# Reordering node work inside the sparse passes of a graph network kernel: when ScalarE stages a node set, and where TensorE's product and transposes stand

## The reference

```python
edge_index = jnp.stack([src, dst])
h = jnp.maximum(_layernorm(x, axis=-1), 0.0)
x = x + _L0_gnn_ref(h, ...)   # twice: concat(h @ W1 + b1, segsum((h @ W0 + b0)[src], dst)) @ W2 + b2, then / std
h = jnp.maximum(_layernorm(x, axis=-1), 0.0)
x = x + _L1_gnn_ref(h, ...)   # segsum(h[src] @ W + b, dst) / clip(deg, 1)
h = jnp.maximum(_layernorm(x, axis=-1), 0.0)
x = x + _L2_gnn_ref(h, ...)   # three graph convolutions, each scaled by 1/sqrt(deg) on both sides
h = jnp.maximum(_layernorm(x, axis=-1), 0.0)
x = x + _L3_gnn_ref(h, ...)   # per edge: relu([h[src], h[dst]] @ Wm1 + bm1) @ Wm2 + bm2, masked, segsum; then a node network
return x
```

## Time and profile before

| | |
|---|---|
| median of 3 runs | 7783.07 us |
| the profiled execution | 7780.93 us |
| its span, first to last instruction | 7779.1 us |
| mean granted TensorE clock | 0.961 of full speed |
| PE busy | 6960.1 us (89%) |
| GpSimd busy | 5398.6 us (69%) |
| VectorE busy | 3609.6 us (46%) |
| ScalarE busy | 1612.6 us (21%) |
| dense matmuls L2451 | 27930, 3617.2 us busy |
| gathers L837 | 3295, 3140.2 us busy |

### The profile page before, as it was taken

The page is one execution under the profiler, slowest core; times in us unless marked ns, Lnnn a source line. Parts: engine busy times, 40 slices in busy tenths (PEclk is TensorE's granted clock), DMA queues, the critical chain, the costliest instruction groups (busy, mean ns, idle before and its releaser), DMA issues.

```text
span 7779.1 us, 139548 instructions
## 1 busy us (share of the span) xinstructions
PE 6960.1 (89%) x53778; PEld 5623.6 (72%) x53778; DVE 3609.6 (46%) x7497; ACT 1612.6 (21%) x3217; POOL 5398.6 (69%) x5559
## 2 busy tenths in 40 slices
PE   2999999899989999999999999999987777777787
PEld 1677777787777777777877777777766666666676
DVE  7888988334442333333322333333344444444444
ACT  4777777111110000000000000010111111111111
POOL 0466666677657777677767777677747777777776
PEclk9999999999999999999999999999988999899898
DMA  7334333666565666655665556666545555555554
GB/s 152 116 129 133 132 123 132 187 191 188 182 200 185 198 196 192 206 183 181 191 207 179 185 186 188 205 193 187 185 154 148 146 146 148 143 151 145 149 144 131
DMA packets 568381, 1306.54 MB, mean 168 GB/s; under 512 B 223636, under 2 KB 326359, under 8 KB 560471
## 3 DMA queue, kind: packets, MB, share of 16 engines
q1 hardware_dynamic: 295076, 810.67, 31.5%
q0 software_dynamic: 177744, 371.65, 18.5%
q10 hardware_dynamic: 94948, 115.60, 4.3%
HBM read 1097.44 MB, written 207.42 MB: 168 GB/s over the span
## 4 chain that ended last, share of the span: by engine, by line
PE 53%; POOL 19%; issue 8%; DMA 3%; DVE 3%; ACT 0%; ACTq 0%; SPq 0%; DVEq 0%; POOLq 0%
PE PS L2451 41%; POOL GF L826 19%; PE PS L2431 5%; DMA work<-amat 2%; PE PS L2598 1%; PE PS L2297 1%; PE PS L2306 1%; PE PS L2516 1%; PE PS L2438 1%; PE PS L2316 0%; PE PS L2293 0%; PE PS L2457 0%; PE PS L2292 0%; DVE work L1839 0%; PE PS L2295 0%
## 5 line engine op out<-in xcount | busy, mean ns | idle before, releaser
L2451 PE MATMUL PS<-PARTS,work 128*128 128x288 bf16 x27930 | 3617.2, 288 | 66.9 <-issue 44.9
L2451 PEld LDWEIGHTS PS<-PARTS,work 128*128 128x128 fp8e4 x27930 | 2747.0, 99 | 760.2 <-issue 83.0
L837 POOL DMA_INDIRECT GF<-newparts,SRC x1640 | 1563.5, 953 | 687.9 <-issue 493.9
L837 POOL DMA_INDIRECT work<-newparts,SRC x1655 | 1576.7, 953 | 540.6 <-issue 498.3
L826 POOL DMA_INDIRECT GF<-table,SRC x1563 | 1475.0, 944 | 532.5 <-issue 475.7
L821 POOL DMA_INDIRECT GF<-newparts,SRC x659 | 749.9, 1138 | 505.0 <-PE PS L2538 202.1
L2598 PE MATMUL PS<-PARTS,work 128*128 128x289 bf16 x5586 | 999.0, 289 | 0.0
L1190 ACT ACTIVATE work<-PS 128x396 fp8e4<-128x396 f32 x1824 | 865.5, 500 | 290.3 <-PE PS L2516 246.2
L1913 DVE TENSOR_REDUCE FREE<-PS 128x96 f32<-128x288 f32 x415 | 189.7, 457 | 1431.1 <-PE PS L2431 1419.1
L2378 PE MATMUL PS<-work,QW 128*96 128x512 bf16 x1173 | 395.9, 455 | 427.8 <-DMA GF<-table,SRC 388.6
L1839 DVE TENSOR_TENSOR work<-PS,REL 128x1024 bf16<-128x1024 f32 (+1 forms) x611 | 741.3, 1214 | 0.3 <-issue 0.3
(11 more groups left out here) (293 smaller groups left out, 5892.0 us busy)
## 6 DMA issues: line engine op xcount, KB each, us to landing
work<-amat SPq DMA_DIRECT2D x285, 896.0 KB
work<-amat SPq DMA_DIRECT2D x285, 672.0 KB
work<-in_dst_dram SPq DMA_DIRECT2D x195, 512.0 KB
amat<-work SPq DMA_DIRECT2D x57, 1568.0 KB, 5.8
work<-in_edge_attr_dram SPq DMA_DIRECT2D x195, 384.0 KB
GF<-newparts,SRC POOLq DMA_INDIRECT x2299
PARTS<-newparts SPq DMA_DIRECT2D x35, 1008.0 KB, 10.0
work<-newparts,SRC POOLq DMA_INDIRECT x1655
```

Of the source, the lines that this page charges most:

```text
L837: pool.indirect_dma_start(GP[place_of(g)][:, i, :], None, part_rows[a % 2], bass.IndirectOffsetOnAxis(ap=SRC[:, tile:tile + 1], axis=0)).t ...
L2451: last = pe.matmul(PS[:, dense_bank(d), 0:PQ], AB[m][:, jj * WIN:(jj + 1) * WIN].bitcast(FP8), PARTS[:, j * PQ:j * PQ + PQ], start=(j == 0 ...
```

## The change

Four edits, all in the part that passes 1 to 5 share:

1. In ScalarE's loop the units of a slot are taken with the lowest q first. In the six overlap slots the newer unit's staging so stands ahead of the older one's second part and stores. In the pass with "l2c" (pass 5) the older unit's row stores and first part are issued ahead of both.
2. `PRODUCT_AFTER` of pass 1 goes from 1 to 4: the product stands behind the last piece of its slot, not behind the second.
3. In pass 5 VectorE's chain goes from the start of its slot to the place at which TensorE has the product: behind what VectorE does for pieces 0 and 1 of the slot.
4. In pass 5 TensorE's transposes go from the end of slot q = 1 (behind the gathered group) to slot q = 2, behind the second piece.

```diff
-PRODUCT_AFTER = {"l0b": 1, "l1": 1, "l2a": 1, "l2b": 1, "l2c": 1}
+PRODUCT_AFTER = {"l0b": 4, "l1": 1, "l2a": 1, "l2b": 1, "l2c": 1}
 # ScalarE
-            def step(s, phase, q, half, u):
+            def step(s, phase, q, half, u, begun=False):
...
                 if name == "l2c" and q == 3:
-                    store_rows(s, phase, half, u)
-                    first_part(s, phase, half, u)
+                    if not begun:
+                        rows_and_first(s, phase, half, u)
                     second_part(s, phase, half, u)
                     store_parts(s, phase, half, u)
...
                 for t in range(TURNS * SLOTS):
-                    for half, u, q in units_in(t):
+                    units = units_in(t)
+                    if PHASES[a + 1] == "l2c":
+                        for half, u, q in units:
+                            if q == 3:
+                                rows_and_first(S, a + 1, half, u)
+                    for half, u, q in sorted(units, key=lambda unit: unit[2]):
                         if q == 0 and half == 0:
                             act.wait_ge(d_add, a * DB + HEAD + SIDE * (u + 1) + 1)
                         if q == 0 and half == 1:
                             act.wait_ge(f_acc, a * GG + SLOTS * (u + 1) + UNIT_AT - SKIP + 2)
-                        step(S, a + 1, q, half, u)
+                        step(S, a + 1, q, half, u, begun=True)
 # VectorE
+                def first_halves(units):
+                    for half, u, q in units:
+                        if q == 1:
+                            step(S, a + 1, q, False, half, u)
+
                 def slot(t):
...
-                    for half, u, q in units_in(t):
-                        step(S, a + 1, q, False, half, u)
-                    for piece in pieces:
+                    units = units_in(t)
+                    for half, u, q in units:
+                        if q != 1:
+                            step(S, a + 1, q, False, half, u)
+                    if not pieces:
+                        first_halves(units)
+                    for k, piece in enumerate(pieces):
                         d, m = divmod(piece, AC)
                         if m == TURN_AT and d:
                             add_block(d - 1, max(0, t - SKIP))
                         if m == AC - 1:
                             sum_parts(d)
+                        if k == min(PRODUCT_AFTER[PHASES[a + 1]], len(pieces) - 1):
+                            first_halves(units)
 # TensorE
-                if after and (q == 2 and name in ("l1", "l2a", "l2b") or q == 1 and name == "l2c"):
+                if after and q == 2 and name in ("l1", "l2a", "l2b"):
                     turned(phase, half, u)
...
                     for half, u, q in units_in(t):
                         if q == 1:
                             step(S, a + 1, 0, True, half, u)
+                        if q == 2 and PHASES[a + 1] == "l2c":
+                            turned(a + 1, half, u)
```

More of the change, by code:

```diff
@@ L2349, in unit @@
                     for after in (False, True):
+                        if after and q == 2 and PHASES[phase] == "l2c":
+                            turned(phase, half, u)
                         step(s, phase, q, after, half, u)
```

## The result

The changed kernel takes 7731.76 us (median of 6 runs, 7721.56 to 7738.24) against 7781.36 us (6 runs) for the kernel before: a ratio of 0.9935, 95% interval 0.9922 to 0.9948, so 0.65% or some 50 us faster. A second comparison on another occasion gave 0.9930 (0.9916 to 0.9944).

The account below looks back on a forecast made before the run. Took GpSimd's gathers to bound passes 2 to 4 and TensorE passes 1 and 5; 24.7 + 7.9 + 5.8 + 21.9, less 2.5 and 3, plus 3.6 gives 58.4 us, so 7724 us median, range 7707 to 7751.

Parts of the forecast that it names:

- What bounds the passes: Passes 2 to 4 bound by GpSimd's gathers (823 us for 82 groups), passes 1 and 5 by TensorE.
- Pass 1, staging 14.2 us and clock 13.5 us: Pass 1: TensorE's product waits 14.2 us for ScalarE's staging in six places, 13.5 us slower clock behind; both go.
- Edit 3, 7.9 us: Pass 5: TensorE's wait for VectorE's sum over parts, 7.9 us in three places, goes.
- Pass 5, staging 10.5 us: Pass 5: TensorE's wait for ScalarE's staging in the six slots, 10.5 us, goes with edit 1.
- Edit 4, 5.8 us less 2.5 for the turned window: Pass 5: transposes' waits for the chain, 5.8 us, go; the turned window then waits 2.5 us (0 to 6).
- Clock in pass 5, 8.4 us: Pass 5: 8.4 of 10.1 us lost to clock falls hang on waits the change touches, and come back.
- Counts, 3 us: Passes 1 and 5: a faster TensorE waits 3 us (0 to 12) for the counts' DMA.
- Pass 5 as a whole: Pass 5 gives some 30 us, near 843 us from first to last group.
- The 3.6 us for modelled ends: Waits are measured from a matmul's modelled end, so 21 stalls are 0.17 us longer each, 3.6 us more gain.
- The clock's first half: Rival: clock falls aren't the stalls' doing (first half), or new short waits cause them too (second); 7746 us, chance 0.08.
- The rival by which waits only change places: TensorE's next partner, turned window or `halves`, is as late, so nothing measurable: 7775 us or so, chance 0.05.
- The transfers': Rival: transfers (gathered rows, counts) take over in passes 1 and 5, 15.1 us each: 7754 us, chance 0.09.

Follow-up runs that it names:

- filled stalls: Kernel before, with 20 dense matmuls into an unused bank ahead of the product in pass 1's six staging-wait slots: ratio 0.9993, pass 1 840.2 us.
- early load: Changed kernel, but in pass 5 ScalarE issues the next residual load ahead of the second part: 7717.42 us, ratio 0.9916 to the kernel before.

## Why the prediction was right, and where its sizes were off

The forecast was 7724 us and 58.4 us of gain; measured were 7731.76 and 49.6 to 54.7 us in two comparisons. By its own steps:

- **What bounds the passes.** Right. Passes 1 and 5 gained and 2 to 4 didn't, and 30.6 us of extra work in them cost 4 to 6. The 823 us worked out for GpSimd's 82 groups were 6 to 8 above the 815 to 817 that passes 2 to 4 took before; nothing in the sum hangs on it.
- **Pass 1, staging 14.2 us and clock 13.5 us.** Right, and shown apart from each other: pass 1 went from 849.9 to 822.6 us (821 forecast), and filled stalls took 9.7 us off it though the product started no earlier. It was credited to edit 1, with edit 2 at nothing beside it. Each of the two does it alone, so edit 1 is worth just as little beside edit 2.
- **Edit 3, 7.9 us.** The wait is gone, and with edits 3 and 4 alone no other took its place. What edit 3 is worth by itself was not measured.
- **Pass 5, staging 10.5 us.** This is the term that was wrong. I took it as gained, and did not ask what the late product had been hiding. The wait did go, but what came next was the load of the residual, 14.5 us late for the chain, and through the chain the turned window. With edit 1 alone pass 5 gained nothing (876.3 us against 872.6), and on top of edits 3 and 4 it gained 0 to 3 us (846.6 against 843.3 and 846.2). The place for it could be seen: in those slots ScalarE issues the load and the staging one after the other behind the same second part, and the staging alone was moved.
- **Edit 4, 5.8 us less 2.5 for the turned window.** The partner was named rightly, the size wasn't: 11.3 us, beyond the bound of 6, and in six slots, not the four with few pieces. The cause was the load and not the chain's own length: with an early load 1.5 us were left, in three places.
- **Clock in pass 5, 8.4 us.** 5.1 us came back (by the records of the granted clock 20.5 us at the lower level before and 10.2 after, which cost half of their length); the new waits brought three new falls.
- **Counts, 3 us.** The waits for them went from 0.6 to 2.3 us in pass 1 and from 6.8 to 3.2 in pass 5: no cost in all, so this term was 4 to 5 us too high and covered part of what the residual's load took.
- **Pass 5 as a whole.** That it came out at 843.3 us (846.2 in the second profile) where 843 was forecast is luck in part. The turned window took 8.8 us more than its term and the clock gave 3.3 less; the counts gave 3.6 us where a cost was set, and 3.4 us of waits at "issue", which no term had, went as well.
- **The 3.6 us for modelled ends.** Not shown, and not refuted. Its share in pass 1 is six stalls, 1.0 us. Waits and clock by the rows make 27.7 us there, less 1.7 for the longer waits for counts 26.0; measured were 27.3, so there was room for it.
- **Rivals.** The clock's first half is out by the filled stalls: the falls of pass 1 were the stalls' doing. Its second half, that new short waits bring the clock down as well, came true in pass 5 at a smaller size, three falls or 5.1 us. The Trainium skill, page "TensorE: Matmul & The Clock Gate", section "Why this matters for your kernels", which spoke for that rival, warns only of longer gaps than these. This case's traces don't agree: waits of 2.2 to 2.5 us were followed by falls in five places of six, and the measurement decides. The rival by which waits only change places was right for one term, the staging of pass 5 (10.5 us gone, 11.3 new at the turned window), and wrong for the others. The transfers' had a point in kind, a late transfer is what limits pass 5 now, but it is neither the gathers nor the counts. The `halves` are not among the waits of any of these profiles.

## What to carry to other kernels

When a wait is removed, the next one need not be where the trace shows a wait today. Here it was among the things that are issued behind the same instruction as the one that was now early. List those, DMA issues included, and ask of each when its reader wants it. Of two edits for one stall look which is enough alone: a place in a table did as much here as a new order. And where TensorE stalls for some 2 us at a time, count the slower clock behind the stall as a likely cost of its own; in pass 1 it was about as large as the stall, in pass 5 before about a third of the waits that the change touched (8.4 against 24.2 us), and behind some stalls it was nothing.

## What the runs showed of the hardware

- Six stalls of 2.2 to 2.5 us cost 14.2 us of waiting and 13.5 us of lower clock; five of the six had a fall behind them. Filling them with matmuls kept the clock at 2.4 GHz.
- The length of a stall doesn't decide it. In pass 5 before, stalls of 1.80 us at the product had a fall behind them (5151.78 and 5228.0 us). In the changed kernel's two profiles of pass 5 the falls stand behind waits of 2.18, 2.70 and 2.71 us and of 2.36, 2.38 and 2.63, while the longest of all, 2.77 us in the second, left the clock whole; so did one of 3.17 us in pass 5 of edit 1 alone, and 2.3 us for counts in the version with the early load.
- GpSimd issues an indirect gather of 128 rows every 1.25 us (0.955 and 0.30 us) where nothing holds it, also with 10 us of matmuls more in each pass: 815 to 820 us for 82 groups in most profiles of passes 2 to 4.
- The load of 240 KB for the residual could be used 4.5 us after its issue (5658.69 to 5663.15 in slot 81 of the changed kernel).
